# Splitting 512-column projection products into two of 256 and moving one pass's tiles by 32 bytes, in an adaLN block of gated linear attention and a channel mix

## The reference

```python
h = layernorm(x) * (1 + ca) + sa
q, k, v = h @ Wq.T, h @ Wk.T, h @ Wv.T            # 512 -> 1024, 16 heads of 64
k = k * sigmoid(h @ Wg.T)
g = -softplus(h @ Wd.T + bd)                      # one log decay per head
s_t = exp(g_t) * s_{t-1} + k_t^T v_t;  o_t = q_t s_t
a = rmsnorm(o) * norm_w * sigmoid(h @ Wog.T)
x = x + ga * (a @ Wo.T)
h = layernorm(x) * (1 + cb) + sb
xr, xk = mix(h, h shifted by one token)
x = x + gb * sigmoid(xr @ W_r.T) * (relu(xk @ W_k.T)**2 @ W_v.T)
```

## Time and profile before

| | before |
|---|---|
| median of 3 runs | 3953.74 us (3952.8 to 3953.86) |
| span of the profiled execution, first to last instruction | 3951.8 us |
| time around that span, by the runs | 1.0 to 2.1 us |
| PE busy | 3838.5 us (97%), 25765 matmuls |
| DVE busy | 2917.6 us (74%) |
| ACT busy, POOL busy | 1338.1 us (34%), 1040.8 us (26%) |
| mean granted clock of TensorE | 0.991 |

### The profile page before, as it was taken

The page is one execution under the profiler, slowest core; times in us unless marked ns, Lnnn a source line. Parts: engine busy times, 40 slices in busy tenths (PEclk is TensorE's granted clock), DMA queues, the critical chain, the costliest instruction groups (busy, mean ns, idle before and its releaser), DMA issues. The chain is left out here.

```text
span 3951.8 us, 74486 instructions
## 1 busy us (share of the span) xinstructions
PE 3838.5 (97%) x25765; PEld 3482.7 (88%) x25765; DVE 2917.6 (74%) x6102; ACT 1338.1 (34%) x3039; POOL 1040.8 (26%) x1427
## 2 busy tenths in 40 slices
PE   7999999999999999999999999699999999999998
PEld 7999999999999999999999999578888888888887
DVE  6777777777777777777777777756667667667666
ACT  3333333333333333333333333333333333333332
POOL 0333443333344333334433433300000000000000
PEclk8999999999999999999999999899999999999999
DMA  3000000000000000000000000421111111121110
GB/s 123 20 21 19 24 20 19 24 19 20 19 24 20 19 24 19 20 19 24 20 19 24 19 20 14 143 72 53 67 66 53 62 70 53 59 72 55 56 69 29
DMA packets 125037, 156.91 MB, mean 40 GB/s; under 512 B 7712, under 2 KB 73264, under 8 KB 124992
## 3 DMA queue, kind: packets, MB, share of 16 engines
q1 hardware_dynamic: 124992, 156.31, 11.9%
HBM read 105.95 MB, written 50.33 MB: 40 GB/s over the span
## 5 line engine op out<-in xcount | busy, mean ns | idle before, releaser
L651 DVE RECIPROCAL gate<-gate 128x256 f32<-128x256 f32 x256 | 448.8, 1753 | 8.8
L1200 POOL TENSOR_TENSOR bn_norm_rstd<-bn_norm_var_eps,c_minus_half 128x2 f32<-128x2 f32 x95 | 80.3, 857 | 1279.7 <-DVE bn_norm_var_eps L1081 1266.7
L804 POOL TENSOR_TENSOR tick<-c_zeros 128x1 f32<-128x1 f32 x256 | 57.1, 223 | 1133.2 <-ACT decay L577 1133.2
L790 POOL TENSOR_TENSOR r_hi<-g_hi,c_upto 128x512 fp32r<-128x512 f32 x256 | 272.7, 1065 | 208.4 <-DVE g_lo L733 208.4
L55 PE MATMUL psJ<-h_hi,w_g_hi 128*128 128x256 f32 x1024 | 313.6, 306 | 13.2 <-DVE h_lo L643 13.2
L665 DVE TENSOR_TENSOR q_lo<-q,q_hi 64x256 fp32r<-64x256 f32 x512 | 305.9, 597 | 11.4
L577 ACT ACTIVATE decay<-psA 128x512 f32<-128x512 f32 x256 | 153.6, 600 | 451.7 <-PE psA L448 451.7
L55 PE MATMUL psJ<-h_hi,w_q_hi 128*128 128x256 f32 x1024 | 305.9, 299 | 0.0
L556 ACT COPY q<-psJ 128x256 f32<-128x256 f32 x256 | 95.4, 373 | 610.0 <-PE psJ L57 610.0
L57 PE MATMUL psJ<-h_hi,w_g_lo 128*128 128x256 f32 x1024 | 288.5, 282 | 0.0
L57 PE MATMUL psJ<-h_hi,w_q_lo 128*128 128x256 f32 x1024 | 288.1, 281 | 0.0
(11 more groups left out here) (247 smaller groups left out, 11940.0 us busy)
## 6 DMA issues: line engine op xcount, KB each, us to landing
o_rows_dram<-o SPq DMA_DIRECT2D x256, 128.0 KB, 1.8
o_rows<-o_rows_dram SPq DMA_DIRECT2D x32, 1024.0 KB, 4.8
an_norm_x<-in_L_attn_x_dram SPq DMA_DIRECT2D x32, 512.0 KB, 3.4
bn_norm_x<-in_L_attn_x_dram SPq DMA_DIRECT2D x32, 512.0 KB, 3.6
x<-in_L_attn_x_dram SPq DMA_DIRECT2D x32, 512.0 KB, 4.4
out_dram<-r_gate SPq DMA_DIRECT2D x64, 256.0 KB, 2.0
s_stage<-in_L_wmod_dram SPq DMA_DIRECT2D x4, 1024.0 KB, 7.5
p_stage<-in_L_attn_Wq_dram SPq DMA_DIRECT2D x2, 1024.0 KB, 5.5
```

The source lines that it names most:

```text
L651: nc.vector.reciprocal(gate[:, 2, :], gate[:, 1, :]).then_inc(s["gate2"], 1)
L790: last = nc.gpsimd.tensor_tensor(dst[:, :, :, :], gg.unsqueeze(3).to_broadcast([P, NC, 2, CH]), t["upto"][:, :].unsqueeze(1).unsqueeze(1). ...
L1200: nc.gpsimd.tensor_tensor(rstd[:, which, :], var_eps[:, which, :], t["minus_half"][:, 0:NC], ALU.pow).then_inc(done, 1)
```

## The change

Each product with 512 moving columns in `project` (kind v) and in `rows_product` is done as two with 256: all blocks of the contraction for columns 0 to 255 into the first half of the bank, then all blocks again for columns 256 to 511 into the second half. The stationary operand of each block is loaded once for each half. The waits in `ready` are taken in the first half only. The 512-column matmuls of `psA` stay. A tile `lead` of 32 bytes, which nothing reads or writes, is asked for ahead of `hT` in pass 1; by the program's allocation every tile of pass 1 from `hT` on now begins at a multiple of 64, and `h_hi`, `h_lo`, `q_hi`, `q_lo`, `r_hi` and `r_lo` at one of 128. The weights and pass 2's tiles stay where they were.

```diff
         x = norm["x"]
+        sb("lead", [P, 8])
         hT = sb("hT", [P, KD, T])
...
                 if kind == "v":
-                    c, half = b % 2, b // 2
-                    hh, hl = (a[:, k, c * CH:(c + 1) * CH] for a in (h_hi, h_lo))
-                    wh, wl = (a[:, k, half * 512:(half + 1) * 512] for a in W["v"])
-                    last = three_passes(nc, bank[:, :], hh, hl, wh, wl, k == 0, k == KD - 1)
-                else:
-                    wh, wl = (a[:, k, b * P:(b + 1) * P] for a in W[kind])
-                    last = three_passes(nc, bank[:, 0:T], wh, wl, h_hi[:, k, :], h_lo[:, k, :], k == 0, k == KD - 1)
+                    continue
+                wh, wl = (a[:, k, b * P:(b + 1) * P] for a in W[kind])
+                last = three_passes(nc, bank[:, 0:T], wh, wl, h_hi[:, k, :], h_lo[:, k, :], k == 0, k == KD - 1)
+            if kind == "v":
+                c, half = b % 2, b // 2
+                for at in range(0, 512, T):
+                    for k in range(KD):
+                        hh, hl = (a[:, k, c * CH:(c + 1) * CH] for a in (h_hi, h_lo))
+                        wh, wl = (a[:, k, half * 512 + at:half * 512 + at + T] for a in W["v"])
+                        last = three_passes(nc, bank[:, at:at + T], hh, hl, wh, wl, k == 0, k == KD - 1)
             last.then_inc(s["proj"], 1)
...
-            for k in range(blocks):
-                for at, eng, sem, value in ready:
-                    if at == k:
-                        eng.wait_ge(sem, value)
-                ah, al = (a[:, k, c * CH:(c + 1) * CH] for a in (a_hi, a_lo))
-                wh, wl = (a[:, k, half * 512:(half + 1) * 512] for a in w)
-                last = three_passes(nc, bank[:, :], ah, al, wh, wl, k == 0, k == blocks - 1)
+            for col in range(0, 512, T):
+                for k in range(blocks):
+                    for at, eng, sem, value in ready:
+                        if at == k and col == 0:
+                            eng.wait_ge(sem, value)
+                    ah, al = (a[:, k, c * CH:(c + 1) * CH] for a in (a_hi, a_lo))
+                    wh, wl = (a[:, k, half * 512 + col:half * 512 + col + T] for a in w)
+                    last = three_passes(nc, bank[:, col:col + T], ah, al, wh, wl, k == 0, k == blocks - 1)
             return last
```

## The result

The changed kernel takes 3969.53 us (median of 4, 3968.97 to 3973.41) against 3953.27 us before (4, 3952.31 to 3953.86): a ratio of 1.0043, 95% interval 1.0029 to 1.0058. It is slower by 16 us (0.4%). I had forecast 3901 us, 52 us faster than before; the time lies above even the second case of my forecast, which ended at 3963 to 3965 us, and I had given 0.18 to "slower". Times are medians; two of the twelve executions of run 7's kernel ran at a mean granted clock of 0.59 and 0.69 and took 5898 and 5087 us, and are left out.

A forecast was written before the change was run, and what follows sets the result against it. TensorE, busy for 97% of the span, was taken as the bound through the pace of its matmuls. The terms -45 (offset), -10.4 (v), -28.6 (pass 2) and +31 (kv wait) gave -53 us: 3953.7 to 3901 us, range 3888 to 3915.

The forecast's parts named there:

- second case of my forecast: Rival "A weight streams at the slow pace": split halves at 118.7 ns, line at multiples of 128; 3965 us, chance 0.30.
- Weights are stationary in both, shapes and clock are the same: Pass 1's 118.7 ns against k2's 113.4 in pass 2, laid to the moving tile's offset; saving taken as 5.0 ns.
- The tile, -45 us: Pass 1's g, q and k gain 5.0 ns on 255 matmuls in 32 tiles, -40.8 us, plus -4 us for fp32 products.
- The fp32 products, for which I took -4: Pass 1's small products streaming misaligned tiles might gain between nothing and 10 us; taken as -4 us.
- The stationary operand was on both sides of that line in pass 2 with no difference.: In pass 2, r's stationary operand is on a multiple of 64, o's 32 past, both 233 ns; used for the split's pace.
- The split, -10.4 and -28.6 us: Halves at 113.4 ns save 6.8 ns a pair in pass 1's v (-10.4 us), 6.2 in pass 2 (-28.6 us).
- The kv wait, +31 us: In pass 2, split kv reaches block 3 before DVE's remainder is done: 0.96 us in each of 32 tiles.
- (1): Sign: pass 1's g, q and k start 113.4 ns apart with means near 276.
- (2): Sign: pass 2's kv, o and og at 113.4 ns per 256 columns, or 117 to 119 under the rival at 128.
- (3): Sign: a recurring TensorE wait for DVE L1168's line in kv's tenth matmul, about 0.9 us, 32 times.
- (4): Sign: a tile of pass 1 shorter by 1.7 us, one of pass 2 unchanged within 0.1 us.
- (5): Sign: longer TensorE waits for `g_raw` and `kw`, by 0.1 and 0.2 us.

The follow-up runs named there:

- run 7: The changed kernel with the kv products alone left whole at 512 columns: 3945.2 us, ratio to before 0.9979.
- run 3: The changed kernel with pass 2's h and z parts also moved to multiples of 64: 3954.59 us, ratio to before 1.0001.
- run 4: Kernel without the computation, only stretches of 24 matmuls at four moving and stationary offsets: 256 columns took 113.3 to 120.0 ns, 512 columns 226.7 to 233.5.
- run 9: The kernel before with the 32-byte tile and another ahead of pass 1's weights, nothing split: 3928.23 us, ratio 0.9937.
- the table: Settled steps in run 10 by moving minus stationary start mod 256: 113.3 to 120.0 ns for 256 columns, 226.7 to 234.2 for 512.
- run 1: The kernel before with the 32-byte tile alone, 512-column products kept whole: 3929.56 us, ratio 0.9937.
- run 8: Matmul stretches alone, with one to six fp32 products ahead or fewer stationary columns: 113.3 or 117.8 ns; equal starts 120.0, with 16 or 64 columns 113.3.
- run 2: The changed kernel without the 32-byte tile, so the split alone: 4006.15 us, ratio to before 1.0134.
- run 10: Matmul stretches alone, one stationary tile and sixteen moving ones 0 to 480 bytes behind it: 256 columns 113.3 to 120.0 ns, 512 columns 226.7 to 234.2.

## Why the prediction was wrong

**"Weights are stationary in both, shapes and clock are the same; the moving tiles begin 32 bytes past a multiple of 64 in the first and on a multiple in the second."** This is the step that failed, and both main terms hung on it. The two rows differ in more than that: the operands of pass 1 are 160 apart mod 256 and those of k2 64. I read the moving tile's own offset out of one comparison. Runs 3, 4 and 9 show that the distance counts, and not where either tile stands. By the table, k2's 113.4 of the earlier trace rows isn't even the pace of its offset. It is the better of two that a distance of 64 gives, and it has the other in the change, at the same addresses.

**The tile, -45 us.** Measured -24 (run 1). The distance went from 160 to 192, and less than half of g, q and k then took 113.3 and the rest 117.8. The gain of one such matmul was 2.1 to 2.7 ns in the mean and not 5.0: 8 us in k, 6 in q, 6 in g, and 5 in v, which I had left as it was. The fp32 products, for which I took -4, show no gain that I could find (the L478 group's steps are 109.7 ns before and after).

**"The stationary operand was on both sides of that line in pass 2 with no difference."** True of 512 columns, where 192 and 224 both give 233.3 in the table. It isn't true of 256, where r (192) takes 113.3 and o (224) 118.3. I carried a fact from one shape to the other.

**The split, -10.4 and -28.6 us.** v's distance is 64 with the tile in place: a pair takes 237.2 ns in the mean, against 236.0 for one whole in run 1, which is +2 us and not -10. In pass 2 the saving came in r and kv (-7 us) and was more than lost in og and o (+11) and k2 (+6): +10 us, by the means above, where I had -28.6. A pair of og or o went from 233.0 to 236.4 where I had 226.8. k2 wasn't in my sum at all. "A weight streams at the slow pace", to which I had given 0.30, was nearest in time, 3965 us, by luck, and named what to look for, 117 to 119 ns in o and og. Its cause was wrong: r's and kv's weights, at the same 64 mod 128, streamed at 113.3.

**The kv wait, +31 us.** Right in place, size and count: 0.92 us against 0.96, 32 times, 29 us; and run 7 shows that the time comes back with it.

**The signs I had named:** (1) wrong for more than half of pass 1 (37 to 44% of the steps are at the faster pace); (2) mixed; (3) right; (4) wrong: a tile of pass 1 takes 0.77 us less and not 1.7 (from the end of one `h_lo` wait to the next, 1017.53 to 1093.56 against 1025.32 to 1102.12), and one of pass 2 1.23 more; (5) the wait for `g_raw` grew by 0.04 us a tile and not 0.1, and the one for `kw` shrank by 2.5 us in all, which I can't explain. With the tile alone both grew as forecast in kind, by 2.0 us (`g_raw`) and 1.7 us (`kw`) in all. The sum of what was measured is -25 + 3 + 38 = +16. Of the 69 us between that and my -53, the tile's term holds 20, v's split 13 and pass 2's 39; the kv wait came out 2 lower.

What stays open is why the distances act as they do. That the two operands act on each other is shown by the distances and by run 8's narrow stationary tiles; that it is the stream and the load of the next stationary operand that meet, and where, is only argued. Also open is what fixes the pace at the start of a stretch. In the kernel k2 was fast in all those that left r whole at a distance of 192 (before, runs 1 and 9) and slow in the others (in run 3 its own distance had changed as well). So the split slowed k2, as runs 1 and 2 show, but not by which step.

## What to carry to other kernels

Before you read a pace as the property of one operand, write down all that differs between the two rows, the distance of the two operands' starts among it. One comparison of two stretches isn't a law, and stretches of 24 matmuls with everything else left out can test it in one run. Where products of 512 columns run at 233 ns, try to place the two tiles at equal starts mod 256 before you split them, and where a product is split by columns, count how much sooner it reaches each block that arrives late.

## What the hardware showed that I had not expected

With everything else the same, the distance mod 256 between the starts of the moving and the stationary tile moves a 256-column fp32r matmul between 113.3 and 120.0 ns and one of 512 columns between 226.7 and 234.2 (run 10), and the best distance for the one is a bad one for the other. With 16 or 64 stationary columns the 120.0 becomes 113.3 (run 8). The Trainium skill, page "TensorE: Matmul & The Clock Gate", section "Step-by-step: what each phase is for", says that TensorE reads the two operands through independent ports and that loading the next tile's weights takes no SBUF read bandwidth from the running matmul. The load is indeed overlapped here (weight loads are busy for 95% of the span beside TensorE's 97%), but the 6.7 ns between 128 and 64 stationary columns at equal starts, and the dependence on the distance, show that the two operands aren't independent in time. The measurement decides.

The same stretch, at the same addresses and into the same bank of PSUM, ran at 113.3 and at 117.8 ns by the number of fp32 products ahead, each repeatable (run 8). A kernel's matmul can so get slower by 4% when something ahead of it changes, as k2 did.
